# A mixture-of-experts layer whose tokens are found by table search instead of being scattered

## What is computed

```python
xf = x.reshape(-1, D)                      # 6250 x 256, normalised
gate_logits = xf @ Wg + bg                 # 8 experts
top_w, top_i = jax.lax.top_k(gate_logits, TOP_K)      # TOP_K = 2
top_w = jax.nn.softmax(top_w, axis=-1)
w_dense = jnp.sum(jax.nn.one_hot(top_i, E) * top_w[..., None], axis=1)
for e in range(E):
    h = jax.nn.gelu(xf @ W1[e] + b1[e], approximate=False)      # 256 -> 1024
    out = out + w_dense[:, e:e + 1] * (h @ W2[e] + b2[e])       # 1024 -> 256
```

## Time and profile before

| | us |
|---|---|
| median of 3 runs | 2771.17 |
| lowest and highest run | 2765.76, 2771.25 |
| span of the profiled execution | 2768.1 |
| busy PE / PEld / DVE / ACT / POOL | 2069.7 / 1854.5 / 1559.2 / 975.2 / 1480.2 |

### The profile page before, as it was taken

One profiled execution on the slowest core, in us unless ns is written; L12 is line 12 of the kernel. 1 busy time (PEld: TensorE's weight loads), 2 busy tenths in 40 slices (PEclk: granted clock), 3 DMA queues, 4 the chain that ended last, 5 costly groups with the idle time before them and its releaser, 6 DMA issues. The chain is left out here.

```text
span 2768.1 us, 56379 instructions
## 1 busy us (share of the span) xinstructions
PE 2069.7 (75%) x13133; PEld 1854.5 (67%) x13134; DVE 1559.2 (56%) x4220; ACT 975.2 (35%) x2748; POOL 1480.2 (53%) x1459
## 2 busy tenths in 40 slices
PE   4423218988376788788888888787808999999997
PEld 3323218988355666666666666665708999999997
DVE  4566525655575666666656566666714555555543
ACT  2333216766241111111111111112305656665664
POOL 2167653434106777777777777775672343334323
PEclk9755559999786888888888787878558999999999
DMA  7312243333354444444444444444642333333331
GB/s 188 84 51 79 73 121 103 114 86 108 121 188 106 115 113 113 112 114 113 110 111 112 111 112 111 112 108 105 199 134 72 67 77 45 73 69 69 69 49 22
DMA packets 204140, 279.41 MB, mean 101 GB/s; under 512 B 74634, under 2 KB 158197, under 8 KB 203953
## 3 DMA queue, kind: packets, MB, share of 16 engines
q0 software_dynamic: 82480, 201.42, 27.9%
q1 hardware_dynamic: 120841, 76.64, 10.6%
q10 hardware_dynamic: 776, 0.89, 0.1%
HBM read 202.11 MB, written 78.46 MB: 101 GB/s over the span
## 5 line engine op out<-in xcount | busy, mean ns | idle before, releaser
L1737 POOL DMA_INDIRECT at_G<-h_as,at_idx x850 | 808.9, 952 | 389.9 <-issue 262.4
L1941 PE MATMUL at_pAgg<-at_G,at_OH 128*128 128x260 f32 x1700 | 549.1, 492 | 133.8 <-DVE at_ACC L1789 92.0
L1941 PEld LDWEIGHTS at_pAgg<-at_G,at_OH 128*128 128x128 f32 x1700 | 413.9, 250 | 234.3 <-DVE at_G L1771 149.3
L1262 POOL DMA_INDIRECT out_dram<-e_ob,e_to x108 | 172.8, 1600 | 404.0 <-DMA out_dram<-e_ob,e_to 190.4
L1454 ACT ACTIVATE e_full<-e_pH,g_bias_hidden 128x256 f32<-128x256 f32 x640 | 326.2, 510 | 110.6 <-PE e_pH L1359 92.7
L1881 ACT ACTIVATE at_OT<-at_pTr 128x384 f32<-128x384 f32 (+1 forms) x300 | 125.7, 470 | 668.0 <-PE at_pTr L1926 667.7
L1535 DVE TENSOR_TENSOR e_hT_low<-e_full,e_hT_high 128x256 fp32r<-128x256 f32 x536 | 259.8, 498 | 110.3 <-ACT e_hT_high L1455 109.5
L1357 PE MATMUL e_pH<-e_xT_high,e_WA_high 128*128 128x256 f32 x1072 | 309.7, 289 | 6.4 <-DVE e_WA_low L1530 4.3
L1358 PE MATMUL e_pH<-e_xT_low,e_WA_high 128*128 128x256 f32 x1072 | 304.2, 284 | 0.0
L1359 PE MATMUL e_pH<-e_xT_high,e_WA_low 128*128 128x256 f32 x1072 | 304.1, 284 | 0.0
L1771 DVE TENSOR_TENSOR at_G<-at_G,at_pIds 128x1536 f32<-128x1536 f32 x150 | 249.9, 1666 | 87.6 <-ACT at_pIds L1888 87.6
(11 more groups left out here) (332 smaller groups left out, 3825.8 us busy)
## 6 DMA issues: line engine op xcount, KB each, us to landing
e_xs<-slot_rows_e SPq DMA_DIRECT2D x55, 261.0 KB
e_xs<-slot_rows_e SPq DMA_DIRECT2D x54, 257.0 KB
at_G<-h_as,at_idx POOLq DMA_INDIRECT x850, 2.8
b_rows<-expert_out SPq DMA_DIRECT2D x14, 896.0 KB, 7.2
g_raw_first<-in_L_ffn_W_dram POOLq DMA_DIRECT2D x8, 1024.0 KB, 8.2
g_raw_last<-in_L_ffn_W_dram POOLq DMA_DIRECT2D x8, 1024.0 KB, 6.4
xt_ar<-a_og SPq DMA_DIRECT2D x7, 910.0 KB, 4.4
h_as<-b_og SPq DMA_DIRECT2D x7, 910.0 KB
```

What stands on the lines that cost most here:

```text
L1262: gp.indirect_dma_start(K.out, at, ob[b][:, s, :], None, bounds_check=NODES - 1, oob_is_err=False, compute_op=ALU.add).then_inc(sent[s], 16)
L1737: gp.indirect_dma_start(G[j][:, c, :], None, K.T1, bass.IndirectOffsetOnAxis(ap=idx[j][:, c:c + 1], axis=0)).then_inc(gathered[j], 16)
L1941: last = nc.tensor.matmul(pAgg[:, 0:DIM + 4], OH[j][:, c, :], G[j][:, c, :], start=(j == 0 and c == 0), stop=(j == NJ - 1 and c == CHUNKS[ ...
```

## The change

Routing is a block of its own, `gating`. It scatters nothing: each token's normalised row and its eight expert shares (zero where not chosen) are stored once, in token order, by seven plain transfers of SP (`K.ROWS`), and the residual by one large one. In place of slot numbers three tables stay in SBUF: for each expert and node tile, how many tokens come before the tile (`K.SPAN`), the running count inside the tile (`K.LOOK`, in bf16), and the rank at which each slot tile begins (`K.RANK0`). They are made after the last batch by ten small bf16 products on PE and some DVE operations.

In the expert stage each tile is searched for five tiles ahead (`AHEAD`). `tile_spans` on DVE marks which node tile each of 256 slots lies in and copies the expert's part of `K.LOOK`; `look_up` on PE, two bf16 products of 128 x 129 in the middle of `final(r)`, fetches the counts of that node tile for each slot; `find` on DVE compares and adds them up to the token's number; `hand` writes it as an index; POOL gathers the rows by two indirect transfers (`gather`), behind the scatter of tile r. `x_out(r+2)` moves from the start of trip r to its end, behind `find`. `shares` becomes one copy. SP's loads of the rows go. `setup` makes two more constants. The first mixture keeps its scatters. The core of the diff (left out: the declarations, what `gating` takes over from `project`, and the calls):

```diff
-TO, WHICH, SHARE = DIM, DIM + 1, DIM + 3
-WIDE0, WIDE1 = DIM + 1, DIM + 5
+TO = DIM
+WIDE0, WIDE1 = DIM + 1, DIM + E1
 NODEROWS = TILES * P
 MAXT = -(-NODES // MT)
 CAP = (MAXT + 1) * MT
+AHEAD = 5
 NT = (2 * NODES) // MT + E1 + 2
-BLANK = max(E0, E1) * CAP
+NT1 = NT + AHEAD + 1
+FAR = 1 << 16
+BLANK = E0 * CAP
...
+                sp.dma_start(K.out[0:full, :].rearrange("(t p) c -> p t c", p=P), K.X[:, 0:TILES - 1, :]).then_inc(x_out, 16)
+                sp.dma_start(K.out[full:NODES, :], K.X[0:TAIL, TILES - 1, :]).then_inc(x_out, 16)
+                sp.wait_ge(consts, 4)
+                sp.dma_start(K.ROWS[NODEROWS:NODEROWS + P, :], blank[:, :]).then_inc(rows_out, 16)
+                for i in range(TRIPS):
+                    a = i * BODY
+                    sp.wait_ge(routed, i + 1)
+                    sp.dma_start(K.ROWS[a * P:(a + BODY) * P, :].rearrange("(t p) c -> p t c", p=P), Y[:, a:a + BODY, :]).then_inc(rows_out, 16)
+                sp.wait_ge(x_out, 32)
+                sp.wait_ge(rows_out, (TRIPS + 1) * 16)
...
+                v.wait_ge(consts, 4)
+                v.wait_ge(std_ready, 1)
+                V.reciprocal(rstd[:, :, :], std[:, :, :]).then_inc(rstd_ready, 1)
+                v.wait_ge(rstd_ready, 1)
+                norm(0)
+                for i in range(TRIPS):
+                    if i + 1 < TRIPS:
+                        norm(i + 1)
+                    if i == 0:
+                        v.wait_ge(w_in, 32)
+                    place(i)
+
+                ch.settle()
+                with nc.allow_low_precision("counts up to 49 are whole in this format"):
+                    V.tensor_reduce(column[:, :].rearrange("p (e o) -> p e o", o=1), K.PAIRS[:, :, 0:TILES], AX.X, ALU.add).then_inc(column_made, 1)
+                v.wait_ge(inside_counted, 1)
+                V.tensor_copy(inside[:, :], pC[0:2 * TILES, :, P - 1]).then_inc(inside_kept, 1)
+                v.wait_ge(before_counted, 1)
...
+                ch.mark(V.scalar_tensor_tensor(K.LOOK[:, :, 0:P], pC[0:2 * TILES, :, :], K.half[:, 0:1],
+                                               base[:, :].rearrange("p (e o) -> p e o", o=1).to_broadcast([2 * TILES, E, P]), ALU.mult, ALU.add))
+                v.wait_ge(counted, 1)
+                ch.link(V.tensor_copy(cnt[:, :], pr[:, 0:E]))
...
+                pe.wait_ge(column_made, 1)
+                for e in range(E):
+                    last = nc.tensor.matmul(pC[0:2 * TILES, e, :], K.PAIRS[:, e, :], K.upto[:, :], start=True, stop=True)
+                last.then_inc(inside_counted, 1)
+                nc.tensor.matmul(pr[:, 0:E], K.ones[:, :], column[:, :], start=True, stop=True).then_inc(counted, 1)
+                pe.wait_ge(inside_kept, 1)
+                nc.tensor.matmul(pr[0:2 * TILES, 256:256 + E], tri[:, :],
+                                 inside[0:TILES, :], start=True, stop=True).then_inc(before_counted, 1)
...
+                def gather(t, b, rows):
+
+                    gp.wait_ge(rows_found, t + 1)
+                    if not isinstance(t, int) or t >= 2:
+                        freed(gp, to_ready, t - 1)
+                    gp.sem_inc(passed, 1)
+                    for s in range(SUB):
+                        gp.indirect_dma_start(xs[b][:, s, :], None, K.ROWS, bass.IndirectOffsetOnAxis(ap=rows[:, s:s + 1], axis=0)).then_inc(x_in[b], 16)
+
+                if not deep:
+                    gather(0, 0, first_rows[0])
+                    gather(1, 1, first_rows[1])
                 split_last(0)
                 for w, done, n in (("a", wa_split, NP), ("l", wl_split, NP), ("m", wm_split, 1)):
                     if w != "m" or deep:
@@ -1325,9 +1568,22 @@
                     with begins(gp, 1):
                         next_first(expert(gp, 1))
...
-                with gp.Fori(0, gp.snap(last + 1)) as i:
-                    trip(i, 0)
-                    trip(i, 1)
+                if deep:
+                    with gp.Fori(0, gp.snap(last + 1)) as i:
+                        trip(i, 0)
+                        trip(i, 1)
+                else:
+                    for t in range(2, AHEAD):
+                        gather(t, t % 2, first_rows[t])
+                    with gp.Fori(0, last) as i:
+                        for b in range(2):
+                            trip(i, b)
+                            gather(i * 2 + (b + AHEAD), (b + AHEAD) % 2, rows_of[(b + AHEAD) % 2])
+                    trip(last, 0)
+                    trip(last, 1)
+                    for b in range(2):
+                        gp.wait_ge(x_in[b], gp.snap(last * (16 * SUB) + (AHEAD + 1 - b) // 2 * (16 * SUB)))
+                        gp.sem_inc(passed, 1)
...
+                        if searching and k == HC // 2 - 1:
+                            look_up(t + AHEAD, (b + AHEAD) % 2, found_late)
                     last.then_inc(tile_done, 1)
 
+                def look_up(t, b, pS):
+
+                    pe.wait_ge(tile_of_ready, t + 1)
+                    if isinstance(t, int) and t > 0:
+                        pe.wait_ge(find_done, t)
+                    for s in range(SUB):
+                        last = nc.tensor.matmul(pS[:, s, :], tile_of[b][:, s * P:(s + 1) * P],
+                                                look[b][:, :], start=True, stop=True)
+                    last.then_inc(looked_up, 1)
...
                 def shares(t, b):
 
@@ -1542,18 +1825,46 @@
                         V.tensor_copy(to_all[:, at, :].rearrange("p o s -> p (o s)"), xs[b][:, :, TO]).then_inc(to_ready, 1)
                         return
                     e = expert(v, t)
-                    freed(v, share_ready, t)
-                    V.scalar_tensor_tensor(picked[:, :, :], xs[b][:, :, WHICH:WHICH + 2], K.iota[:, bass.ds(e, 1)], xs[b][:, :, SHARE:SHARE + 2],
-                                           ALU.is_equal, ALU.mult).then_inc(picked_ready, 1)
-                    v.wait_ge(picked_ready, t + 1)
-                    V.tensor_reduce(share[:, at, :].rearrange("p o s -> p (o s)").rearrange("p (s o) -> p s o", o=1),
-                                    picked[:, :, :], AX.X, ALU.add).then_inc(share_ready, 1)
-                    V.tensor_copy(to_all[:, at, :].rearrange("p o s -> p (o s)"), xs[b][:, :, TO]).then_inc(to_ready, 1)
+                    V.tensor_copy(share[:, at, :].rearrange("p o s -> p (o s)"),
+                                  xs[b][:, :, bass.ds(DIM + e, 1)].rearrange("p s o -> p (s o)")).then_inc(to_ready, 1)
+
+                def tile_spans(t, b):
+
+                    at = slice(t, t + 1) if isinstance(t, int) else bass.ds(t, 1)
+                    ch = Chain(v, spanned, t * 2)
+                    e = expert(v, t)
+                    if not isinstance(t, int) or t > 0:
+                        v.wait_ge(tile_of_ready, t)
+                    ch.link(V.tensor_scalar(limits[:, :], K.SPAN[:, bass.ds(e, 1), :].rearrange("p o k -> p (o k)"),
+                                            K.RANK0[0:2 * TILES, at], None, ALU.subtract))
+                    ch.link(V.tensor_scalar(reached[:, :], K.slot[0:2 * TILES, :], limits[:, 0:1], None, ALU.is_ge))
+                    V.tensor_copy(look[b][:, :], K.LOOK[:, bass.ds(e, 1), 0:P + 1].rearrange("p o n -> p (o n)"))
+                    V.scalar_tensor_tensor(tile_of[b][:, :], K.slot[0:2 * TILES, :], limits[:, 1:2], reached[:, :], ALU.is_lt, ALU.mult).then_inc(tile_of_ready, 1)
+
+                def find(t, pS):
+
+                    at = slice(t, t + 1) if isinstance(t, int) else bass.ds(t, 1)
+                    ch = Chain(v, search, t * (SUB + 1))
+                    v.wait_ge(looked_up, t + 1)
+                    for s in range(SUB):
+                        ch.mark(V.tensor_scalar(lower[:, s, :], pS[:, s, 0:P], K.RANK0[:, at], K.token[:, s:s + 1], ALU.subtract, ALU.is_le))
+                    ch.settle()
+                    ch.link(V.tensor_reduce(place[:, :].rearrange("p (s o) -> p s o", o=1), lower[:, :, :], AX.X, ALU.add))
+                    V.scalar_tensor_tensor(found[:, :], pS[:, :, P], float(NODEROWS), place[:, :], ALU.add, ALU.add).then_inc(find_done, 1)
+                    v.wait_ge(find_done, t + 1)
+
+                def hand(t, rows):
+
+                    at = slice(t, t + 1) if isinstance(t, int) else bass.ds(t, 1)
+                    V.tensor_scalar(to_all[:, at, :].rearrange("p o s -> p (o s)"), found[:, :], float(NODEROWS), None, ALU.min)
+                    V.tensor_scalar(rows[:, :], found[:, :], float(NODEROWS), None, ALU.min).then_inc(rows_found, 1)
 
                 def o_out(t, b):
...
+                    if begin and begin != "last" and not searching:
                         x_out(r + (D + 1), (b + D + 1) % 2)
                     if begin:
-                        units(r + D, (b + D) % 2, hT, 0, fh_ready, fl_ready)
+                        early = [(2 * n + 1, n + 2) for n in range(AHEAD - 2)] if not deep and not end else []
```

(27 more changed lines are left out.)

391 lines of the change are left out of this document (285 added, 106 removed).

## The result

The kernel after takes 2851.0 us (median of 4 runs, 2848.0 to 2858.6), the kernel before 2768.5 (4 runs, 2764.9 to 2771.3): a ratio of 1.0303, 95% interval 1.0283 to 1.0323. The profiled execution of after spans 2857.0 us, that of before 2768.1. 5.4 of these 88.9 us lie in attention, which the change does not touch: its end shows in the row in which SP issues the gate's weights.

A forecast was written before the change was run, and what follows sets the result against it. POOL's scatters bounded routing, PE the expert stage. Ordinary trips 35.9, first weights 25.9, POOL 46.1, clock 17, less 6.2: 118.7 us; less 58.6 gained: +60.1 on 2768.1, plus 3.1 to the median: 2831 us, range 2760 to 2885.

The forecast's parts named there:

- the two mechanisms: In the expert stage: DVE's search chain delays PE's `first`, and POOL's lag delays the gathers at expert changes.
- Routing: Last logits at 1991, tables at 2006.7, handover at 2007.5 (bound 2016), the 10.8 us of handover gone.
- Head: Start of the expert stage: first product 2021.8, rows of tile 2 last, at 2039.1; 58.6 us gained up to there.
- Ordinary tile: DVE's 5.6 us chain before `first` makes PE wait 0.77 us; 0.97 us more a tile, 35.9 in 37 trips.
- The perf-mode rule: In `tile_spans`, the skill's rule would make two bf16 operations some 0.15 us cheaper, 3 us over the stage.
- First weights: Seven trips with `lows` before `find`: wait of 3.5 us, with products 3.7 us a trip (2 to 5).
- POOL at a change: Gather behind POOL's split, loads and scatters: PE waits 7.4 us for rows at six changes, 44.4 us.
- Clock: PE's granted clock falls after waits: 1.3 us lost at each of 13 waits, 17 us (0 to 26).
- The 6.2 us: PE's old waits for split weights at expert changes, taken off because they fall into the longer waits.
- the cover holds: Rival for the expert stage: chain and gathers fit, only PE's products remain; -48, 2723 us, chance 0.13.
- ACT's lag does not shrink: Rival: each wait counts in full, another 0.9 us in 37 trips, 2864 us, chance 0.15.
- both middle rivals: Only POOL's lag bites, 2775 us, chance 0.10; or only DVE's chain doesn't fit, 2785 us, chance 0.10.

The follow-up runs named there:

- e1: Kernel after with `x_out` back at the front of DVE's trip and PE's `first` waiting for `find`; ratio to before 1.0164, 910.5 us behind attention.
- e7: e5 with `tile_spans` of the next look-up placed before `o_out`; ratio to before 0.9969, 830.7 us behind attention.
- e11: Kernel after with the subtraction of the last weights' split moved from POOL to DVE; ratio to before 1.0192, 924.0 us behind attention.
- e4: Kernel after with `tile_spans` ahead of the low parts, PE's look-up waiting for the last low part; ratio to before 1.0112, 882.3 us behind attention.
- e2c: Kernel after with POOL's gather ahead of weight loads and scatter only where the expert changes; ratio to before 1.0222, 904.0 us behind attention.
- e6: Kernel after with each of PE's look-ups done twice; ratio to before 1.0296, 919.4 us behind attention.
- e5: Kernel after with e1, e4 and e2 together and the look-up in the banks of units 2 and 3; ratio to before 0.9926.
- e10: e7 with the subtraction of the last weights' split moved from POOL to DVE; ratio to before 0.9783, run again 0.9883.
- e2: Kernel after with POOL's gather behind the split and ahead of loads and scatter in every trip; ratio to before 1.0292, 946.0 us behind attention.

## Why the prediction was right, point by point

The median is 2851 us, forecast 2831, inside the range of 2760 to 2885, and the two mechanisms that it names for the loss are there. By medians the change costs 83 us, forecast 60. What follows compares the two profiled executions; that of after was the longest of its four runs.

- **Routing.** Counted from attention's end: last logits 64.9 us (predicted 64.7), end of the tables 80.3 (80.4), handover 81.1 (81.2). The stores did not bound it, and the 10.8 us of handover are gone.
- **Head.** First product 96.2 us behind attention's end (95.5), turn of tile 2 115.1 (112.8). Here the size was right by luck, since the reason was wrong. The rows of tile 2 were not last: POOL had issued their gather by 2038.5, and there is no wait at 2046.80. The look-ups in PE's first tile were, with 4.9 and 3.6 us of waiting. That tile took 18.9 us where the prediction had 13: it took no account of the further step that `tile_spans` comes behind `find` in DVE's list, 6.8 us from look-up to look-up. The gain is 56.3 us (58.6).
- **Ordinary tile.** Last low part T + 1.8 (T + 1.7), chain of 5.5 us (5.6), wait of 0.77 (0.77), 13.2 us a tile (13.0). The step that the wait in the middle of `final` is covered held for the kernel after; e1 shows how thin the cover is. Above 12.0 the 26 ordinary trips lost 1.2 us each, 31 us, and eleven trips behind the long ones 2.1 us each, 23: 54 us against 35.9. These eleven are of two kinds. Six stand directly behind a wait for rows; in them PE hardly waits and its granted clock is 0.82 to 0.88 (the row below), so their length is the clock's, which the sum has as a term of its own. The other five follow at a clock of 1.00, and PE waits 0.6 to 1.0 us for `tile_of` besides the 0.6 to 0.8 for `x_out`. That was no term of the sum; in the one that I looked at, `tile_of` ends T + 4.5 instead of T + 3.6, and what delays it was not traced further.

```profile
2250.63:2265.07 14.44, 14.44 (x102) 0.82 0.26 39
```

- **The perf-mode rule.** The four operations of `tile_spans` took 0.26, 0.29, 0.20 and 0.48 us where 0.2, 0.3, 0.2 and 0.45 were priced without the rule. The Trainium skill, "VectorE: DVE Perf Modes", "The perf-mode tier table (the rule you actually need)", would by the prediction's estimate have them 0.15 us shorter in all, and against these prices no such gain shows. But the 0.3 was read from no row of a comparison: in the same tile a reduce of 256 elements takes 0.42 us and the fourth operation, with two operands of 256, 0.48, against 0.29 for the comparison. So this run does not speak against the rule.
- **First weights.** The wait is 3.4 to 3.6 us (3.5), in six trips and not in seven: at the fifth change DVE's `lows` fall in the trip behind a wait for rows, in which PE runs at a granted clock of 0.83 and does not wait for them. A trip with this wait is 5.2 us longer than an ordinary one (4.0 with the clock): the difference is the clock, below. e1 and e7 show the same trips at 17.2 and 12.7 us in the mean.
- **POOL at a change.** The rows arrive 25.9 us after F (27.0). A trip takes 20.2 us, predicted 19.6 and 1.3 for the clock. The term of 7.4 us was right as a sum and wrong in its parts: 3.0 us fall in the middle of `final`, where DVE's low parts stand behind POOL's subtraction and `tile_of` behind them, and 3.2 to 4.4 in the turn. e11 takes most of the first part away and the second grows to 5.9; in e4 PE comes to it earlier, with 2.4 to 2.9 us left of the first, and the second grows to 7.1. The lag is POOL's, as predicted; e2c takes it away.
- **Clock.** A term that was too small. After the 3.5 us before 2461.91 the granted clock is 0.50, the lower of the two levels, for four microseconds and more, where the earlier trace rows had shown 0.65:

```profile
2461.90:2466.00 4.10, 4.09 (x19) 0.50 0.01 0
2466.00:2470.00 4.00, 4.00 (x31) 0.83 0.30 32
```

  19 products where 36 fit: `first` takes 8.2 us instead of 5.76, after 2143.43 it takes 7.1. That is 1.4 to 2.4 us a wait instead of 1.3. The price is not a fixed one: e6 has two such waits, and e2c one, after which the granted clock stays at 1.00 and the trip takes 15.8 to 16.2 us. After the waits for rows it falls in the next trip, the six named above.
- **The sum.** 136.4 us of loss in the stage against 118.7: ordinary and following trips 18 more, part of it clock; the thirteen long ones 4 more (93.3, against 89.0 for fourteen, waits and clock together); less 5 that the old stage's own waits and first tile make. The 6.2 us that the prediction takes off for them is PEld's wait; the trips of the old stage were 9.2 us over 12.0 each in all, and its first tile was 2.0 longer than the new one's. There are 56.3 of gain against 58.6, 3.4 us behind the last turn that no step had, and 5.4 of attention in this one execution. The 3.1 us between span and median, which the prediction adds, came from two different executions: the profiled execution of after took 2858.6 us with a span of 2857.0, 1.6 more.
- **Rivals.** That the cover holds was far off. That ACT's lag does not shrink is excluded by T + 1.8; its price was also too high, since 1.5 and 0.2 make 1.7 us a tile and not 1.9. In both middle rivals one of the two mechanisms is missing; both are there.

## What to carry to other kernels

When work is taken from a stage and put into a loop, price it by the place in the longest dependent chain of the loop, not by the idle time of its engine. DVE was idle 6.3 of 12.0 us in each tile, and still a chain of 5.5 us, where 3.9 lay between its last low part and PE's next `first`, cost 1.2 us in each tile; with 1.8 us of it done ahead of the low parts (e4) it costs 0.1. A queue that was allowed to lag because nobody read what it made (POOL's scatters) becomes the bound as soon as a read is put behind it; put reads ahead of what nobody waits for, but only there, and look what else the queue held. When two waits in one chain lie close together, removing one shows the other.

## What the runs showed of the hardware that was not expected

- POOL's subtraction of 128x1024 elements takes 2.45 us, and an operation of DVE with two operands in SBUF that begins beside it ends 0.3 us behind it: `o_out` took 3.02 us instead of 0.88, seven low parts 7.45. DVE does the same subtraction in 1.2 us. A comparison of 98x256 bf16 elements with one operand in SBUF took 2.44 us instead of 0.29. The Trainium skill, "SBUF — State Buffer", "Who interferes with whom", says that a DVE instruction with two inputs in SBUF contends with a POOL instruction that reads SBUF, and that one in a two-port mode locks it out, or is locked out, for the whole instruction; the traces agree, and the comparison behaves as the page has it for a two-port mode. The prediction weighed this rule only against the gathers, where it gave nothing, and not against the split beside which the new operations could come to lie; in the kernel after they don't, in e5 they do.
- Beside an unbroken row of DVE's operations with two operands in SBUF, POOL's indirect transfers get longer. In e5, where low parts often follow each other without a gap, 21 of 101 scatters took 2.25 to 2.94 us instead of 1.63; in the kernel after, where 0.3 us lie between them in most tiles, none of 101 is longer than 1.84. In e10 three gathers took 5.2 us instead of 1.0, each beside low parts and the two subtractions of the split in one row. One of them:

```profile
2646.31 5.21 POOL L1564 DMA_INDIRECT e_xs<-gate_rows,e_rows_of  x1 [0.30 <-issue]
...
2646.96 2.35 DVE L1822 TENSOR_TENSOR e_WL_low<-g_raw_last,e_WL_high 128x1024 fp32r<-128x1024 f32 x2
2649.23 1.42 DVE L1830 TENSOR_TENSOR e_hT_low<-e_full,e_hT_high 128x256 fp32r<-128x256 f32 x4
```

- The pauses of ACT in e2, 1.5 us at the end of a scatter, have no explanation here.
